# GRU recurrence in a graph network: ten time steps instead of two in the body of TensorE's loop

## The reference, cut to what matters

```python
def gru(x_seq, W_ih, W_hh, b_ih, b_hh):
    H = W_hh.shape[1]                      # 512
    pre_i = x_seq @ W_ih.T + b_ih
    def step(h, pi):
        ph = h @ W_hh.T + b_hh
        r = jax.nn.sigmoid(pi[:H] + ph[:H])
        z = jax.nn.sigmoid(pi[H:2 * H] + ph[H:2 * H])
        n = jnp.tanh(pi[2 * H:] + r * ph[2 * H:])
        h_new = (1.0 - z) * n + z * h
        return (h_new, h_new)
    _, ys = jax.lax.scan(step, jnp.zeros((H,)), pre_i)   # 1250 steps
```

## Time and profile before

| | |
|---|---|
| median of 3 runs | 5085.2 us |
| lowest, highest | 5081.38, 5090.95 us |
| the profiled execution's own time | 5089.79 us |
| its span (first to last instruction) | 5087.7 us |
| TensorE busy (matmuls) | 4957.9 us, 97% of the span |
| VectorE, ScalarE, GpSimd busy | 57%, 38%, 17% |
| the recurrence (first to last matmul of L494) | from 698.9 to 3950.6 us, 3252 us |

### The profile page before, as it was taken

The page is one execution under the profiler, slowest core; times in us unless marked ns, Lnnn a source line. Parts: engine busy times, 40 slices in busy tenths (PEclk is TensorE's granted clock), DMA queues, the critical chain, the costliest instruction groups (busy, mean ns, idle before and its releaser), DMA issues.

```text
span 5087.7 us, 337016 instructions
## 1 busy us (share of the span) xinstructions
PE 4957.9 (97%) x131794; PEld 4250.1 (84%) x131795; DVE 2880.4 (57%) x16350; ACT 1950.7 (38%) x15372; POOL 846.6 (17%) x5071
## 2 busy tenths in 40 slices
PE   7899999999999999999999999999999999999989
PEld 7765579999999999999999999999999445555554
DVE  6551346666666666666666666666666525445551
ACT  0111025555555555555555555555555101222110
POOL 0000012222222222222222222222222000000000
PEclk9999999999999999999999999999999998999989
DMA  1011210000000000000000000000000100011011
GB/s 61 0 70 68 102 38 0 0 0 0 0 0 0 0 0 0 0 0 0 0 0 0 0 0 0 0 0 0 0 0 0 59 17 19 18 36 36 22 51 42
DMA packets 28932, 81.11 MB, mean 16 GB/s; under 512 B 1594, under 2 KB 1834, under 8 KB 28858
## 3 DMA queue, kind: packets, MB, share of 16 engines
q1 hardware_dynamic: 28858, 80.03, 4.3%
HBM read 58.08 MB, written 21.95 MB: 16 GB/s over the span
## 4 chain that ended last, share of the span: by engine, by line
PE 94%; DVE 2%; issue 2%; DVEq 1%; ACT 0%; POOL 0%; DMA 0%; ACTq 0%; SPq 0%; POOLq 0%
PE psum L494 64%; PE psum L567 8%; PE psum L363 5%; PE psum L353 4%; PE psum L579 4%; PE psum L411 3%; PE psum L476 2%; PE psum L553 2%; PE psum L643 2%; DVE r L880 1%; PE psum L426 0%; PE psum L458 0%; DVEq L875 0%; DVE r L879 0%; DVE stat L813 0%
## 5 line engine op out<-in xcount | busy, mean ns | idle before, releaser
L494 PE MATMUL psum<-h,r 128*128 128x16 f16 (+1 forms) x80000 | 3063.3, 181 | 9.1 <-ACT psum L707 4.3
L494 PEld LDWEIGHTS psum<-h,r 128*128 128x128 f16 x80000 | 2670.6, 96 | 39.1 <-DVEq L993 4.9
L494 PE MATMUL psum<-h,hn 128*128 128x16 f16 (+1 forms) x40000 | 2122.2, 177 | 0.0
L494 PEld LDWEIGHTS psum<-h,hn 128*128 128x128 f16 x40000 | 1592.6, 96 | 0.0
L999 DVE TENSOR_TENSOR_SCAN psum<-mul_rz,psum 128x6 f32<-128x6 f32 x5000 | 854.9, 171 | 590.8 <-PE psum L494 542.5
L707 ACT COPY psum<-big 128x2 f32 (+1 forms) x7506 | 1002.8, 163 | 0.0
L315 POOL TENSOR_TENSOR upd_add<-upd,signs 128x4 f32<-128x4 f32 x2500 | 504.2, 202 | 2591.2 <-DVE upd L1018 1832.0
L720 ACT ACTIVATE mul_n<-psum 128x2 f32<-128x2 f32 x2500 | 434.4, 174 | 1177.9 <-DVE psum L999 1177.8
L1018 DVE TENSOR_TENSOR_SCAN upd<-upd_mul,upd_add 128x8 f32<-128x8 f32 x2500 | 417.2, 167 | 300.4 <-ACT upd_mul L725 300.4
L729 ACT ACTIVATE upd_add<-psum 128x2 f32<-128x2 f32 x2500 | 434.1, 174 | 297.4 <-DVE psum L1005 297.4
L1014 DVE TENSOR_TENSOR_SCAN h<-upd_mul,upd_add 128x8 f16<-128x8 f32 x2500 | 425.2, 170 | 169.9 <-POOL upd_add L315 3.8
(11 more groups left out here) (224 smaller groups left out, 2538.1 us busy)
## 6 DMA issues: line engine op xcount, KB each, us to landing
ws<-in_Wl SPq DMA_DIRECT2D x9, 1024.0 KB, 5.4
ws<-in_Wr SPq DMA_DIRECT2D x9, 1024.0 KB, 7.6
edge_counts<-adj SPq DMA_DIRECT2D x2, 3051.8 KB
edge_weights<-big SPq DMA_DIRECT2D x1, 6103.5 KB
adj_rows<-big SPq DMA_DIRECT2D x1, 6103.5 KB
adj<-adj_rows SPq DMA_DIRECT2D x1, 6103.5 KB
big<-edge_counts SPq DMA_DIRECT2D x1, 6103.5 KB
adj<-edge_weights SPq DMA_DIRECT2D x1, 6103.5 KB
```

The lines of the kernel that those rows point to most:

```text
L494: m = mm(places, whh16[g][:, part, 2 * kc + k, (2 * c + j) * P:(2 * c + j + 1) * P], state.unsqueeze(1).broadcast_to([P, COPIES, 2 - part] ...
```

## The change

TensorE's loop runs 125 passes with ten steps in the body, unrolled, where it ran 625 passes with two. The parity `u`, the waits and the matmuls of a step are the same. The loops of VectorE, ScalarE and GpSimd are left as they are, with two steps in the body.

```diff
 COPIES = 16
+STEPS = 10
...
-            with pe.Fori(0, N // 2) as i:
-                for u in range(2):
-                    t = 2 * i + u
+            with pe.Fori(0, N // STEPS) as i:
+                for step in range(STEPS):
+                    t = STEPS * i + step
+                    u = step % 2
                     pe.wait_ge(s("gru_high0"), t + 1)
                     pe.wait_ge(s("gru_put_r0"), t + 1)
                     gru_gate(u, 0, 0, 0, part=1)
```

## The result

Ten steps in the body: **6214.7 us** median of 6 runs (6212.3 to 6224.0) against 5086.5 us before (6 runs); the ratio is 1.2224, 95% interval 1.2207 to 1.2241. The kernel is 22% slower. The forecast was 6150 us, between 5550 and 6950.

What follows compares the result with a forecast made beforehand. TensorE's matmuls were taken to bound the recurrence. Refetching the unrolled body's instructions, less saved branches, summed to 8.6 us per pass, 1075 us in 125 passes; added to 5085 this gave about 6150 us, range 5550 to 6950.

Steps and rivals of the forecast that it cites:

- What bounds the kernel, and that a branch costs 0.10 us: Recurrence: TensorE bounds it at 27.0 ns per matmul with weight load; the body-end branch adds 0.10 us uncovered by queued matmuls.
- Where the blocks lie and how many: TensorE's new body: blocks of 256 instructions begin at 32, 288, 544 and so on; nine touched, a tenth fetched ahead.
- ten is nearer to the second: Holding is proven up to four blocks, not holding from 15; ten is nearer to 15, so the body isn't held (0.80).
- VectorE's case: Expert loops: VectorE's body of 372 instructions, 23 KB, was fetched anew on the second pass, so what is held is small.
- branch target, with the useless block ahead of it: Each pass's branch: fetching its target costs 3.5 us, plus 1.0 us waiting for the unneeded tenth block's fetch.
- second block: After the branch: only 32 instructions (0.43 us) cover the next block's fetch, costing 3.1 us per pass.
- seven borders: Later block borders in the body: 3.45 us of work against a 3.55 us fetch, +0.1 each, +0.7 us per pass.
- slower matmuls: half clock: After gaps the clock falls to 0.5 for 3.4 to 6.8 us per pass, slowing matmuls by 0.7 us in all.
- The wait behind the useless block: At the branch: fetches served one at a time delay the target 0 to 1.95 us behind the tenth block; 1.0 taken.
- Held after all: Recurrence: ten blocks are held, 500 branches of 0.10 us go, giving 5035 us, or up to 5050; chance 0.14.
- Every border pays in full: Body's seven borders: each fetch ahead comes 1.34 us late, costing 9.4 instead of 0.7 us per pass; 7250 us; chance 0.05.
- Nothing to measure: Recurrence: body held, but waits on VectorE and ScalarE replace the branch's 0.10 us pause; 5085 us; chance 0.01.

## Why the prediction was right, point by point

- **What bounds the kernel, and that a branch costs 0.10 us**: right. It is 0.12 us alone and 0.095 us net.
- **Where the blocks lie and how many**: right, to the instruction. Nine blocks and one ahead were forecast, ten packets per pass came. The step "ten is nearer to the second" was an argument from distance and could have gone wrong: the runs put the limit at eight, and the same ten steps, one block fewer and with a hint, were held. VectorE's case, read as "what is held is small", told nothing of TensorE, which holds eight. The Trainium skill (Runtime: NRT & Kernel Launch, section Instruction fetch mechanics) says 2048 instructions in blocks of 256; the runs agree with that as eight blocks, and 1942 instructions, though fewer than 2048, did not fit at their place. That section speaks of a window of two blocks for a taken branch, which the prediction left out; the runs do not bear it out, since bodies that touch three to eight blocks branched back without a packet.
- **The sum per pass.** Before, ten steps took 960 x 27.05 ns = 25.97 us; after, 2000 us held 54714 matmuls, 35.09 us for 960. The excess is 9.1 us (8.6 forecast). (5085 + 1075 is 6160, put down as 6150.) Its terms, as means over 123 passes (without the first and the last) from the starts of the matmuls, beside what was put down:

| term | forecast | measured |
|---|---|---|
| five branches' ordinary cost gone, 0.124 each (forecast: four, 0.10 each) | -0.4 | -0.6 |
| branch target, with the useless block ahead of it | 3.5 + 1.0 | 4.14 |
| second block | 3.1 | 2.56 |
| seven borders | 0.7 | 2.24 |
| slower matmuls: half clock (measured with the inner steps' 0.014 us) | 0.7 | 0.8 |
| sum | 8.6 | 9.1 |

- **The term that was mis-sized** is "seven more borders, +0.1 each". About five of them show a gap, of 0.43 us. The packets start 3.8 us apart (2003.9, 2007.9, 2011.6, 2015.4 us in the trace) and a block's work at full clock is 3.35 us, so the loop runs at the pace of its fetches. The forecast put a fetch at 1.0 + 1.1 + 1.45 = 3.55 us; measured at the last five borders are 1.17 us from the border to the packet's start, 1.25 for the packet and 1.38 to the first instruction, 3.80. A margin of 0.10 us between fetch and work was forecast, and it is 0.45: an error that is nothing beside one long gap, and most of what a border costs. The first of the seven shows no gap, since the block ahead of it takes 3.9 us, with the matmuls behind the two long gaps slower.
- **The wait behind the useless block** was taken as 1.0 us, for fetches served one at a time. The step was wrong in kind. With fifty steps the useless packet starts 1 us earlier and has landed 0.8 us before the target's packet starts, and the gap is 3.5 us; here it has not landed when the target's starts, and the gap is 4.1. The target's packet is not put back by it (it starts 0.68 us behind the last matmul's start here, 0.62 with fifty steps), but it lasts 1.82 instead of 1.15 us. That is the 0.6 us; why the packet is longer no run shows.
- **The clock.** The 3.4 to 6.8 us of work per pass at half clock had no row behind them. The windows view from 1000 to 3000 us has a granted clock of 0.87, from which I estimate 9 us of 35 at the lower level, part of them idle. The cost came out near: 0.8 instead of 0.7 us.
- **Luck.** The borders were forecast 1.5 us too low, the gap behind the branch 0.4 and the second block's 0.5 us too high. They cancel in part, so the total is closer than its parts, and that is luck.
- **The rivals.** "Held after all" would have been right with the body 32 instructions further on and a hint: 5055 us, near its 5035. "Every border pays in full" (7250 us) was out: a border costs 0.3 us on average, and the stop of 1.34 us had come with the DMA engines 0.97 busy, where they are 0.02 busy here. "Nothing to measure" was out too; whatever the waits on the state take, it is at most 0.014 us per step, not 0.10.

## What to carry to other kernels

Count a loop's body in fetch blocks at the place where it lies, with the one block behind it, not in bytes: TensorE held eight of 16 KB in all, and 1554 instructions gave a gain of 0.8% where 1942 cost 22%. Unrolling pays per branch removed (0.095 us here), so most of it comes early: four steps gave 26 us, eight, the version to use, 40. A body that fills its eight blocks needs the hint on its branch, and of the two bodies beyond the store the very long one lost less (5542 us with fifty steps, 6215 with ten).

## What the runs showed of the hardware that I had not expected

- A block behind the loop's end, which is never run, cost 650 us: 5708 us without the hint and 5055 with it, for the same ten steps in eight blocks.
- That fetch is a race with the branch. One instruction in the last block never caused it, thirteen (1.8 us) did so in 65 of 155 passes, 118 and 150 in every one.
- The packet of the branch's target lasted 1.82 us where it started before the useless one had landed, 1.32 us where that one had landed 0.4 us before (ten steps at the border), and 1.15 us where it had landed 0.8 us before (fifty steps).
- Twelve semaphore increments at the end of a body are 0.15 us apart and leave TensorE without matmuls for 1.8 us, some fifteen times an ordinary branch.
